# Layer norm in four batches, query units begun on two row blocks, last row block finished in two column halves

## What is computed

```python
xn = layernorm(x)
qkv = xn @ w_qkv.T
scores = einsum('bskgd,btkd->bkgst', qh, kh) * scale      # causal mask, softmax
attn = einsum('bkgst,btkd->bskgd', probs, vh)
s = attn.reshape(...) @ w_dense.T
h = relu(s0 * (xn @ sign(k0))) * 2.0
h = relu(ei_dense(h, k1, s1)) * 2.0
g = silu(ei_dense(h, k2, s2))
out = x + s * g
```

## Time and profile before

| | |
|---|---|
| median of 3 runs | 915.73 us |
| profiled execution | 917.22 us, of which the span of the trace is 915.1 us |
| TensorE busy | 896.1 us, 98% of the span, 4272 matmuls and transposes |
| VectorE busy | 677.7 us, 74% |
| ScalarE busy | 513.2 us, 56% |
| GpSimd busy | 463.3 us, 51% |
| mean granted TensorE clock | 0.997 |

### The profile page before, as it was taken

How to read it: one execution, slowest core, us unless ns; L and a number is a source line. 1 busy time by engine, 2 the same in 40 slices (tenths; PEclk the granted TensorE clock), 3 DMA queues, 4 the chain that set the end, 5 groups by cost and what they waited for, 6 DMA issues and landing times.

```text
span 915.1 us, 15937 instructions
## 1 busy us (share of the span) xinstructions
PE 896.1 (98%) x4272; PEld 757.4 (83%) x4272; DVE 677.7 (74%) x1163; ACT 513.2 (56%) x1077; POOL 463.3 (51%) x372
## 2 busy tenths in 40 slices
PE   7999999999999999999999999999999999999997
PEld 6878778888788878888788887888788887888886
DVE  7768767787677867788667876788677786678865
ACT  3656645665466645666356644666456663555633
POOL 5246443564346635555336634465445563355775
PEclk9999999999999999999999999999999999999999
DMA  6496655857386764865577573867549664655472
GB/s 218 121 249 192 132 115 156 241 132 152 66 239 197 155 120 115 244 165 118 103 192 222 136 155 61 243 185 153 109 127 255 157 124 86 171 151 125 103 202 86
DMA packets 204806, 143.58 MB, mean 157 GB/s; under 512 B 23152, under 2 KB 172144, under 8 KB 204784
## 3 DMA queue, kind: packets, MB, share of 16 engines
q1 hardware_dynamic: 176112, 129.68, 55.9%
q10 hardware_dynamic: 28672, 13.64, 6.9%
HBM read 63.70 MB, written 23.20 MB: 95 GB/s over the span
## 4 chain that ended last, share of the span: by engine, by line
issue 51%; POOL 30%; PE 14%; DMA 2%; SPq 1%; DVE 1%; POOLq 1%; ACT 0%; DVEq 0%
POOL pt_lo L767 21%; POOL w_lo L777 6%; POOL wd_lo L777 3%; PE ps_m L1251 3%; PE ps_s L1236 2%; PE ps_o L1119 1%; PE ps_o L1121 1%; PE ps_o L1120 1%; PE ps_m L1119 1%; PE ps_m L1120 1%; PE ps_m L1121 1%; PE ps_s L1120 1%; PE ps_s L1121 1%; PE ps_s L1119 1%; SPq L674 1%
## 5 line engine op out<-in xcount | busy, mean ns | idle before, releaser
L767 POOL TENSOR_TENSOR pt_lo<-pt_lo,pt_hi 128x512 fp32r<-128x512 f32 x248 | 326.2, 1339 | 257.6 <-ACT pt_hi L866 257.6
L959 DVE CUSTOM_DVE_ANT_0 ps_s<-ps_s,mask 128x32 f32<-128x32 f32 (+31 forms) x256 | 181.8, 716 | 93.7 <-PE ps_s L1121 92.2
L866 ACT ACTIVATE pt_hi<-pt_lo 128x512 fp32r<-128x512 f32 x288 | 172.6, 628 | 78.7 <-PE ps_o L1121 42.8
L1119 PE MATMUL ps_m<-xn_hi,w_hi 128*128 128x512 f32 (+1 forms) x388 | 152.2, 392 | 1.8 <-DVE q_lo L1067 1.8
L1121 PE MATMUL ps_m<-xn_hi,w_lo 128*128 128x512 f32 (+1 forms) x388 | 150.9, 389 | 0.0
L1120 PE MATMUL ps_m<-xn_lo,w_hi 128*128 128x512 f32 (+1 forms) x388 | 150.8, 389 | 0.0
L819 ACT ACTIVATE prob_even<-ps_s,small 128x32 f32<-128x32 f32 (+15 forms) x128 | 82.8, 648 | 99.5 <-DVE small L959 98.1
L819 ACT ACTIVATE prob_odd<-ps_s,small 128x160 f32<-128x160 f32 (+15 forms) x128 | 96.1, 754 | 63.1 <-DVE small L959 36.4
L1120 PE MATMUL ps_s<-k_lo,q_hi 128*128 128x480 f32 (+15 forms) x384 | 126.6, 330 | 0.0
L1121 PE MATMUL ps_s<-k_hi,q_lo 128*128 128x480 f32 (+15 forms) x384 | 126.5, 329 | 0.0
L1119 PE MATMUL ps_s<-k_hi,q_hi 128*128 128x480 f32 (+15 forms) x384 | 124.7, 325 | 0.0
(11 more groups left out here) (100 smaller groups left out, 1429.5 us busy)
## 6 DMA issues: line engine op xcount, KB each, us to landing
raw<-wqkv SPq DMA_DIRECT2D x48, 256.0 KB, 4.3
pt_lo<-prob_odd SPq DMA_DIRECT2D x96, 128.0 KB, 3.9
pt_lo<-prob_even SPq DMA_DIRECT2D x96, 112.0 KB, 3.2
pt_lo<-prob_odd SPq DMA_DIRECT2D x96, 96.0 KB, 2.7
raw<-wd SPq DMA_DIRECT2D x32, 256.0 KB, 4.1
inv_rows<-inv SPq DMA_DIRECT2D x32, 256.0 KB, 4.2
at_lo<-inv SPq DMA_DIRECT2D x32, 256.0 KB, 3.4
turned<-prob_odd SPq DMA_DIRECT2D x32, 256.0 KB, 4.1
```

Of the source, the lines that this page charges most:

```text
L767: pool.tensor_tensor(pt_lo[:, slot, :], pt_lo[:, slot, :].bitcast(F32), pt_hi[:, hi_slot, :], ALU.subtract).then_inc(land_lo, 1)
L866: act.activation(pt_hi[:, hi_slot, :], pt_lo[:, LAND_AT[i] + j, :].bitcast(F32), ACT.Copy).then_inc(land_hi, 1)
L959: dve.tensor_tensor_reduce(out=scores, in0=scores, in1=mask[:, S - width(i % BLOCKS, tile):S], scale=-1.0, scalar=BIG, op0=ALU.add, op1=AL ...
L1119: pe.matmul(out, sta_hi, mov_hi, start=start, stop=False)
```

## The change

The layer norm is taken in four batches of two blocks instead of two of four. The root for a batch waits for the variances alone: ScalarE adds `eps` as the bias of its root, and makes minus half of `var + eps` as well; a root of a constant zero stands ahead, and four small memsets on VectorE make the constants. GpSimd's low parts of `q0`, `q2` and `k` wait until 2, 4 and 6 blocks are scaled. TensorE turns blocks 0 and 1, makes the first column halves of `q0` and of `q1` (`begin`), turns blocks 2 and 3, makes the second halves, then `q2`, `q3`, blocks 4 and 5, `k`, blocks 6 and 7, `v`. The warm-up has 25 transposes instead of 36. ScalarE splits `q2`, `q3`, `k` and `v` one at a time between its other work.

At the end, `gate.7` and the addition of `x` for block 7 no longer wait for its last product; TensorE makes that product in two column halves, in the two banks, and VectorE multiplies and adds each half (four instructions of 256 columns); SP stores the two halves apart.

```diff
-WARM_UP = 36
+WARM_UP = 25
+BATCHES = BLOCKS // 2
+SPLIT_AFTER = {"q0": 2, "q2": 4, "k": 6}
...
-    pe = ln(0, 1, 2, 3) + unit("q0") + unit("q1") + unit("q2") + ln(4, 5) + unit("q3") + ln(6, 7) \
-        + unit("k") + unit("v") + [("scores", first, r) for r in tiles] + values
+    pe = ln(0, 1) + [("begin", "q0"), ("begin", "q1")] + ln(2, 3) + unit("q0")[-1:] + unit("q1")[-1:] + unit("q2") \
+        + unit("q3") + ln(4, 5) + unit("k") + ln(6, 7) + unit("v") + [("scores", first, r) for r in tiles] + values
...
-    act = [("root", 0)] + hi(split[0], split[1], *ln(0, 1, 2, 3), *split[2:], units[0]) \
-        + [("root", 1)] + hi(units[1], units[2], *ln(4, 5), units[3], *ln(6, 7), units[4])
+    root = [("root", n) for n in range(BATCHES)]
+    act = [("root_table",)] + root[:1] + hi(split[0], split[1], *ln(0, 1)) + root[1:2] + hi(*ln(2, 3), split[2], units[0]) \
+        + root[2:3] + hi(units[1], split[3], units[2]) + root[3:] + hi(split[4], units[3], *ln(4, 5), split[5], units[4]) \
+        + hi(*ln(6, 7))
...
-    dve = stats[:4] + [("moments", 0)] + scaled[:4] + lo(*ln(0, 1, 2, 3)) \
-        + stats[4:] + lo(units[0]) + [("moments", 1)] + lo(units[1]) + scaled[4:] \
-        + lo(units[2], *ln(4, 5), units[3], *ln(6, 7), *units[4:]) + [("ffn_scales",)]
+    dve = stats[0] + moments[:1] + rooted[:1] + scale[0] + stats[1] + lo(*ln(0)) + moments[1:2] + lo(*ln(1)) \
+        + rooted[1:2] + scale[1] + lo(*ln(2, 3)) + stats[2] + moments[2:3] + lo(units[0]) + rooted[2:3] + scale[2] \
+        + lo(units[1]) + stats[3] + moments[3:] + lo(units[2]) + rooted[3:] + scale[3] \
+        + lo(units[3], *ln(4, 5), units[4], *ln(6, 7), units[5]) + [("ffn_scales",)]
...
-        lo.weigh.6 gate.4 gate.5 lo.land.7.7 mul.weigh.7 lo.weigh.7 lo.dense.6 gate.6 lo.dense.7
-        gate.7 add_x.7
+        lo.weigh.6 gate.4 gate.5 lo.land.7.7 mul.weigh.7 lo.weigh.7 lo.dense.6 gate.6 gate.7 add_x.7
+        lo.dense.7
...
+                        if kind == "prologue" and piece in SPLIT_AFTER:
+                            pool.wait_ge(xn_ready, SPLIT_AFTER[piece])
...
-                        half = slice(item[0] * 4, item[0] * 4 + 4)
-                        act.wait_ge(ln_step, LN_STEPS * item[0] + 1)
-                        act.activation(std[:, half], var_eps[:, half], ACT.Sqrt).then_inc(ln_sqrt, 1)
+                        half = slice(item[0] * 2, item[0] * 2 + 2)
+                        act.wait_ge(ln_moments, 2 * item[0] + 2)
+                        act.activation(std[:, half], mv[:, half, 1], ACT.Sqrt, bias=eps).then_inc(ln_sqrt, 1)
+                        act.activation(half_var[:, half], mv[:, half, 1], ACT.Identity, scale=-0.5, bias=half_eps)\
+                           .then_inc(ln_sqrt, 1)
...
+                    elif name == "dense" and kind == "last" and item[1] == BLOCKS - 1:
+                        i = item[1]
+                        gate = silu[i % SILU_RING]
+                        for part, cols in enumerate(HALVES):
+                            dve.wait_ge(shared_done, r.shared_no(item) + part)
+                            dve.tensor_tensor(gate[:, cols], last_bank(r, part)[:, cols], gate[:, cols], ALU.mult)\
+                                .then_inc(last_row_scaled, 1)
+                            dve.wait_ge(last_row_sum, 1)
+                            dve.wait_ge(last_row_scaled, part + 1)
+                            dve.tensor_tensor(y[:, i, cols], y[:, i, cols], gate[:, cols], ALU.add)\
+                                .then_inc(last_row_ready, 1)
...
+            def unit_of_blocks(piece, bank, part):
+
+                w = PIECES.index(piece)
+                cols = slice(part * HALF // 2, (part + 1) * HALF // 2)
+                for n in range(CHUNKS):
+                    mm = three(bank[:, cols], (w_hi[:, w, n, :], w_lo[:, w, n, :]),
+                               (xn_hi[:, n, cols], xn_lo[:, n, cols]), n == 0, n == CHUNKS - 1)
+                return mm
```

More of the change, by code:

```diff
@@ L459, in build @@
         mask = sb("mask", [P, S], BF16)
-        small = sb("small", [P, 3 * STAT_RING + 9])
+        small = sb("small", [P, 3 * STAT_RING + 13])
         neg_max, row_sum, row_inv = (small[:, n * STAT_RING:(n + 1) * STAT_RING] for n in range(3))
@@ L463, in build @@
         credit, inh_mul, inh_add = (small[:, n:n + 1] for n in range(3 * STAT_RING + 6, 3 * STAT_RING + 9))
+        zero, minus_one, eps, half_eps = (small[:, n:n + 1] for n in range(3 * STAT_RING + 9, 3 * STAT_RING + 13))
         bn = vt[:, 0:48].rearrange("p (b n) -> p b n", n=6)
         mv = vt[:, 48:64].rearrange("p (b n) -> p b n", n=2)
-        var_eps, std, rstd, half_var, newton = (vt[:, 64 + 8 * n:72 + 8 * n] for n in range(5))
+        std, rstd, half_var, newton = (vt[:, 64 + 8 * n:72 + 8 * n] for n in range(4))
         inv_rows = sb("inv_rows", [P, HEADS * P])
@@ L546, in shared_bank, with last_bank @@
             return ps_m[run.place(item) % 2] if item in run.order else None
+        def last_bank(run, part):
+            return ps_m[(run.place(("dense", BLOCKS - 1)) + part) % 2]
         x_loaded = [sem(f"x_loaded{b}") for b in range(BLOCKS)]
@@ L996, in run @@
                         continue
+                    if what == "rooted":
+                        rooted(item[0])
+                        continue
                     if what == "scale":
                         b, = item
[L999 removed]
+                        dve.wait_ge(ln_step, LN_STEPS * (b // 2 + 1))
                         dve.tensor_scalar(x_sb[:, b, :], x_sb[:, b, :], mv[:, b, 0:1],
@@ L1128, in _, with second_block_pair @@
                 pe.transpose(ps_m[0][:, 0:P], ident[:, :], ident[:, :])
+            def unit_of_blocks(piece, bank, part):
[5 more added lines that the diff above has]
+                return mm
+            def second_block_pair(piece, bank):
+                pe.wait_ge(ln_lo, 4)
+                return unit_of_blocks(piece, bank, 1)
             def run(kind, g):
@@ L1186, in run @@
                         w = PIECES.index(piece)
-                        if kind == "prologue" and no == 1:
-                            for cols in (slice(0, HALF // 2), slice(HALF // 2, HALF)) if c == 0 else ():
-                                pe.wait_ge(ln_lo, cols.stop // P)
-                                for n in range(CHUNKS):
-                                    mm = three(bank[:, cols], (w_hi[:, w, n, :], w_lo[:, w, n, :]),
-                                               (xn_hi[:, n, cols], xn_lo[:, n, cols]),
-                                               n == 0, n == CHUNKS - 1)
+                        if kind == "prologue" and no <= 2:
+                            mm = second_block_pair(piece, bank)
                         else:
@@ L1201, in run @@
                             mm.then_inc(shared_done, 1)
+                    elif name == "begin":
+                        piece = item[1]
+                        pe.wait_ge(w_split, r.piece_no(piece))
+                        pe.wait_ge(ln_lo, 2)
+                        unit_of_blocks(piece, ps_m[r.place(("unit", piece, 0)) % 2], 0)
                     elif name == "vblocks":
@@ L1217, in run @@
                                 pe.wait_ge(w_split, r.piece_no(f"wd{HEADS - 1}"))
+                        if kind == "last" and i == BLOCKS - 1:
+                            for part, cols in enumerate(HALVES if h == HEADS - 1 else ()):
+                                if part:
+                                    pe.wait_ge(shared_read, r.shared_no(whole(item)) - 1)
+                                for n in range(HEADS):
+                                    mm = three(last_bank(r, part)[:, cols], (at_hi[:, i % ATTN_RING, n, :],
+                                                               at_lo[:, i % ATTN_RING, n, :]),
+                                               (wd_hi[:, n, cols], wd_lo[:, n, cols]), n == 0, n == HEADS - 1)
+                                mm.then_inc(shared_done, 1)
+                            continue
                         mm = three(bank[:, :], (at_hi[:, i % ATTN_RING, h, :],
```

53 lines of the change are left out of this document (32 added, 21 removed).

## The result

| | kernel before | changed kernel |
|---|---|---|
| median (12 runs each, same chip) | 915.85 us | 919.89 us |
| lowest to highest | 914.21 to 919.06 | 916.28 to 921.59 |
| profiled execution: time | 917.22 us | 921.16 us |
| its span | 915.1 us | 919.4 us |

The ratio of the two kernels, taken over all their runs, is 1.0037, with a 95% interval of 1.0023 to 1.0051; the two medians alone give 1.0044. The change makes the kernel slower by 0.4%, 3.4 to 4.0 us, and the time lies above the range of the prediction (912.5 to 917.2). It stays under 920.3, so the case "same", to which the prediction gave 0.93, is the one that came, but the forecast gain of 1.25 us did not.

What follows compares the result with a forecast made beforehand. TensorE, busy 98% of the span, was taken to bound the kernel, so only its two ends counted. Start -1.45 and end +0.2 gave -1.25 us, from 915.73 to 914.5 us; range 912.5 to 917.2.

Steps and rivals of the forecast that it cites:

- case "same": Whole kernel: time stays between 911.1 and 920.3 us, not distinguishable from no change (about 0.5%); chance 0.93.
- forecast gain of 1.25 us: Whole kernel: -1.45 us at the start plus 0.2 at the end, giving 914.5 us; chance 0.45.
- +0.7: Start, first half of `q0`: 0.7 us gained if TensorE's granted clock stays at 1.00 instead of falling to 0.50.
- about 1.0 us of cover lies there, and 0.5 costs nothing: Fifth score tile, 36.04: about 1.0 us of slack before TensorE waits, so maxima slipping 0.5 us cost nothing.
- landing forecast for 33.4: Scale loads: last one issued at 27.1 behind the fill, landing 6.3 us later at 33.4, against a need at 32.9.
- Rival 4: Scales and fill land 3 us later still, maxima at 36.4, 2.5 us lost beyond cover: 917.0 us; chance 0.07.
- Rival 1: Start: TensorE's clock falls to 0.50 anyway, costing 1.5 us; scores at 33.6, no gain, 915.9 us; chance 0.27.
- First product: Start: TensorE's first product begins at 11.05 instead of 14.54, 3.5 us sooner.
- New stall: Start, behind the turning of blocks 2 and 3: TensorE waits 1.7 us before the second halves.
- Scores: End of the start section: first scores at 32.15 us, 1.45 us sooner than before.
- The end: Last row block: VectorE's chain ends at 913.04, 0.4 later; smaller store lands 0.2 sooner; net +0.2 us.
- rival 3: End: block 7's addition stands until GpSimd's is done; 0.85 later, less 0.2 for the store, 914.9 us; chance 0.13.

Runs made afterwards that it cites:

- fifth run: Changed kernel with TensorE kept busy by filler transposes in its two gaps, scale loads left late: 916.67 us, 1.0010 of the kernel before.
- seventh run: Changed kernel with the old end restored (last row block as one 512-column product and one store): 918.02 us, 1.0025 of the kernel before.
- sixth with late scales: Changed kernel with 36 warm-up transposes instead of 25, scale loads left late: 918.02 us, 1.0034 of the kernel before.
- run 2: Kernel before with the three scale loads issued right behind the load of k: 916.12 us, 1.0002 of the kernel before.
- run 3: Kernel before with one added wait, so SP issues the scale loads only when unit v is made: 917.9 us, 1.0034 of the kernel before.
- run 8: Kernel before with the change's new end alone: 915.13 us, 1.0000 of the kernel before.
- run 11: The changed kernel measured once more, nothing edited: 919.59 us, 1.0038 of the kernel before.
- run 1: Changed kernel with the three scale loads issued right behind the load of k: 916.58 us, 1.0013 of the kernel before.
- fourth run: Changed kernel with scale loads early and filler transposes behind blocks 1 and 3 (18 and 12): 914.25 us, 0.9990 of the kernel before.
- second of the sixth: Changed kernel with scale loads early and 36 warm-up transposes instead of 25: 916.13 us, 1.0012 of the kernel before.
- tenth run: Changed kernel with early scale loads, filler transposes in both gaps, and block 7's gate and addition ahead of block 6's: 913.9 us, 0.9980 of the kernel before.

## Why the prediction was wrong

**The steps that failed** are two, and the ratios behind the fifth run give them about equal weight. One is the term "+0.7" for a clock that stays: the clock fell, and the scores came at 34.55 instead of 32.15, 2.40 late (its parts are below). The other is "about 1.0 us of cover lies there, and 0.5 costs nothing", behind a landing forecast for 33.4: the landing came 3.7 late, and there was less cover. By the ninth score tile the late scales have added 1.60 us to the 0.95 by which the scores themselves are later than before.

- *The cover.* I read it at 36.04, the first place where TensorE takes a bank that an exponential frees, and stopped there. At that place the first exponential ended 2.83 later (37.88 instead of 35.05) and TensorE was 1.98 later, so the cover was 0.85. At the ninth tile, which needs the bank of the exponential of 160 columns, there was none. TensorE and ScalarE of the kernel before:

```profile
38.89 0.40 PE L1119 MATMUL ps_s<-k_hi,q_hi 128*128 128x288 f32 x1
```

```profile
38.35 0.39 ACT L819 ACTIVATE prob_odd<-ps_s,small 128x160 f32<-128x160 f32 x1
```

  ScalarE was done at 38.74 and TensorE began 0.15 later. In the changed kernel TensorE begins at 41.44, again 0.15 after the end of this:

```profile
40.89 0.40 ACT L840 ACTIVATE prob_odd<-ps_s,small 128x160 f32<-128x160 f32 x1
```

  Here 2.54 us of lateness give 2.55 at TensorE. The other traces with late scales and no fall of the clock near the scores agree: the doubling of the scales was 3.16, 3.03 and 0.59 late (seventh run, the sixth with late scales, and the fifth), and the ninth tile 3.00, 2.88 and 0.44.
- *The wait at 54 us.* The same maxima feed a longer chain: exponential, transposition, store to memory, landing of the turned rows, ScalarE's next work, the split of `q`, and TensorE. TensorE, and ahead of it ScalarE, of the kernel before:

```profile
54.42 0.50 PE L1119 MATMUL ps_m<-xn_hi,w_hi 128*128 128x512 f32 x1 [1.35 <-DVE q_lo L1067]
```

```profile
52.46 0.61 ACT L819 ACTIVATE prob_odd<-ps_s,small 128x416 f32<-128x416 f32 x1 [5.65 <-DMA turned<-prob_odd]
```

  The same two in the changed kernel stand at 57.48, shown above, and here:

```profile
55.52 0.61 ACT L840 ACTIVATE prob_odd<-ps_s,small 128x416 f32<-128x416 f32 x1 [4.14 <-DMA turned<-prob_odd]
```

  From these two traces alone it looks as if the lateness passed through memory in full, 3.06 us. The other traces do not bear that out, since the time through the chain differs between executions:

| trace | doubling of the scales | exponential of 416 columns | between | TensorE's wait for `q_lo` |
|---|---|---|---|---|
| before | 34.41 | 52.46 | 18.05 | 1.35 |
| before, scales early (run 2) | 34.73 | 51.29 | 16.56 | none |
| before, scales late (run 3) | 37.54 | 54.20 | 16.66 | none |
| before, new end (run 8) | 33.92 | 51.83 | 17.91 | 1.21 |
| changed | 37.11 | 55.52 | 18.41 | 1.85 |
| changed, again (run 11) | 37.11 | 55.20 | 18.09 | 1.55 |
| changed, scales early (run 1) | 36.79 | 53.32 | 16.53 | none |

  The second and the fourth row have the start of the kernel before, and only one of them has the wait. So this chain can take or give 1.5 us in a single trace; what decides it no run tested, and whether late scales lengthen it stays open.
- *The landing.* Forecast 33.4, while VectorE got the scales at 37.11, 3.7 later. `k`'s low part ends at 27.59 instead of 25.2: 2.4, the same as TensorE is late (scores at 34.55 instead of 32.15). Another 1.0 was my misreading: I took the scale issued at 21.59 for the last one, but it was the second of three. SyncE's queue of the kernel before from 22 us on, and of the changed one from 31 us on:

```profile
21.59 2.49 SPq L648 DMA_DIRECT2D small<-s  x2
```

```profile
30.50 1.45 SPq L665 DMA_DIRECT2D small<-s  x1
```

  The last scale is issued at 30.50, 2.9 behind `k`'s low part where I had put 1.9, and 6.6 us lie from there to VectorE, where I had put 6.3. With this one reading right, the forecast's own sum would have given 34.4 and a slip of 1.5 in place of 0.5.

**Rival 4** is the case that happened. It put the decision at a landing of 35.3, and the loss at what exceeds 1.0 us of cover; the mechanism was right, the chance of 0.07 far too low, and its cover too large, 1.0 where the ninth tile left none. (By its own terms it decides from 35.2 on, not 35.3: 32.9, the cover of 1.0 and the gain of 1.25.) What it "hangs on" I had listed, ScalarE's turn among it, without noticing that this turn depends on TensorE's own speed.

**Rival 1** happened with it. I put it at 0.27 and gave it "no gain"; it cost 0.95 at the scores. But I treated the two as alternatives, each with a sum of its own, although the slower clock is what makes the scales late. Separate chances are wrong where one rival feeds another: the case of both together had no sum and no chance.

The rest of the start, by its steps:

- *First product* at 11.31, forecast 11.05 (3.23 gained of 3.5): right.
- *New stall*: forecast 1.7, measured 1.57 in front of 18.35: right.
- *Clock*: forecast +0.7 for a clock that stays. It was at 0.50 from 11.5 to 14.9. The 24 matmuls of the first halves took 15.74 - 11.31 = 4.43 us; at full clock, 14.00 - 11.05 = 2.95 (fourth run). So the fall costs 1.48 here, where TensorE is full. Before, it had cost the 0.7 of the forecast: from the first product to the scores the kernel before took 33.60 - 14.54 = 19.06, and the kernel of the eighth run, with the same start and no fall in its trace, 33.11 - 14.73 = 18.38. (The row at 14.54 reads 0.55, not the 0.56 that I wrote; nothing hangs on it.)
- *Scores* at 34.55 instead of 32.15, 2.40 late: 0.26 is the first product, 1.48 the clock, and 0.66 is left, since the fourth run, with its first product at 11.05 exactly and the clock held, came to 32.81. Some 0.2 of it stand by 16.61 (11.05 + 24 x 0.12 + 0.8 + 1.7 = 16.43); the rest lies in the units behind, where that trace shows no wait, and I did not separate it.

**The end**: forecast 913.04, 0.4 later than before by a gate and an addition that GpSimd hinders at 1.05 each. Measured 0.36 later relative to the last product, by another way: the gate was not hindered at all and the addition stood for the whole of GpSimd's, which is rival 3's mechanism; it had put +0.85, with the addition ending 911.69 - 910.32 = 1.37 after the last product, while it ended 913.60 + 1.59 - 914.24 = 0.95 after it. The Trainium skill, SBUF — State Buffer, section Who interferes with whom, says that a VectorE instruction with two SBUF inputs and a GpSimd instruction that reads SBUF exclude each other for the whole of the one that came first. The rows of 1.60 on GpSimd and 1.59 on VectorE agree. The start of the changed kernel shows it too: L974, an operation on two columns that takes 0.16 in its neighbours, took 1.20 beside `k`'s low part:

```profile
26.21 0.16 DVE L971 TENSOR_TENSOR vt<-vt 128x2 f32<-128x2 f32 x1
26.41 1.20 DVE L974 SCALAR_TENSOR_TENSOR vt<-vt 128x2 f32<-128x2 f32 x1
```

The "net +0.2 us" of the end is neither confirmed nor refuted by the times: the end alone measured 1.0000 with an interval of 1.2 us to each side.

**What stays open.** From the unit that waits for `q_lo` to the end of the last product nothing is changed, yet that stretch takes 855.9 us before, 856.8 and 856.1 in the two traces of the changed kernel, and from 854.0 to 857.1 in those of the other runs. Executions differ by 3 us there, so single traces settle nothing smaller, and the 0.9 that the changed kernel loses after 57 us can be this alone. What makes this variation I did not test.

## What to carry to other kernels

When a step is moved later, walk down every queue that waits for it, and look at the small items at its far end: here three loads of 0.5 KB stood behind a gated load and a fill of 1,792 KB, and were needed before both. Cover has to be sought at each later place that the same chain feeds, not at the first one only: here it was 0.85 us at the fifth score tile and nothing at the ninth, where the trace before showed no wait, but an exponential that ended 0.15 before TensorE began. A wait seen in one trace may be absent in the next one of the same code, so a cover or a loss that rests on it needs a second trace. An idle stretch should be priced with the clock at both levels: what falls behind it is not only the matmuls, but whatever waits for them. Work that does not need the last product belongs ahead of the product before it as well, in an idle stretch of the engine, and clear of the other engine's addition.

## What the hardware showed that I had not expected

- The granted clock of TensorE falls at a time that differs between executions of the same kernel: at 0.50 from 11.5 to 14.9 us in one trace of the changed kernel and from 12.3 to 15.7 in the other. With other small edits it was 10.8 to 17.6 (first run) or did not fall at all before the end (second of the sixth, and the eighth, whose start is that of the kernel before, where it fell from 12.7 to 16.1). With the gaps filled it was at 1.00 in all three traces taken (fourth, fifth and tenth run).
- Three loads of 0.5 KB behind a fill of 1,792 KB took 6.4 us to land, while a 256 KB load ahead of the fill took 2.7.
- A wait of TensorE of 2.21 us in the middle of its work was followed by a clock of 0.50 from 39.5 to 43.0 us (third run), which began 1.1 us after TensorE had started again.
- The path from the doubling of the scales through memory to the exponential of 416 columns took from 16.53 to 18.41 us in the traces of the table above, where TensorE's instructions between are the same.
